# Attention in a four-layer transformer sequence: softmax sums as columns of the values matmul, division by query

## The reference

```python
attn = jnp.einsum('bhnd,bhsd->bhns', q, k) * SCALE
attn = jax.nn.softmax(attn, axis=-1)
o = jnp.einsum('bhns,bhsd->bhnd', attn, v)
return o.transpose(0, 2, 1, 3).reshape(B, N, D)     # then @ proj_w + proj_b
```

## Time and profile before

| what | value |
|---|---|
| median of 3 runs | 2044.21 us |
| the profiled execution | 2036.93 us |
| its span, first to last instruction | 2035.2 us |
| PE (matmul) busy | 1920.9 us, 94%, 40741 instructions |
| PEld (weight load, beside PE) busy | 1591.5 us, 78% |
| DVE busy | 1685.4 us, 83%, 3915 instructions |
| ACT busy | 1411.7 us, 69%, 3672 instructions |
| POOL busy | 648.7 us, 32% |
| mean granted TensorE clock | 0.994 of full speed |

### The profile page before, as it was taken

The page is one execution under the profiler, slowest core; times in us unless marked ns, Lnnn a source line. Parts: engine busy times, 40 slices in busy tenths (PEclk is TensorE's granted clock), DMA queues, the critical chain, the costliest instruction groups (busy, mean ns, idle before and its releaser), DMA issues.

```text
span 2035.2 us, 93251 instructions
## 1 busy us (share of the span) xinstructions
PE 1920.9 (94%) x40741; PEld 1591.5 (78%) x40741; DVE 1685.4 (83%) x3915; ACT 1411.7 (69%) x3672; POOL 648.7 (32%) x1132
## 2 busy tenths in 40 slices
PE   3789999999999999999999999999999999999998
PEld 2567878887877887878887877887888887777877
DVE  2778888888888898878898888898888888889875
ACT  1455767777776777776777776777776777676777
POOL 1322333333333323333323333333333332323322
PEclk9899999999999999999999999999999999999999
DMA  4200000000000000000000000000000000000000
GB/s 176 53 3 3 16 21 21 21 11 18 21 16 21 21 21 11 19 16 21 21 20 10 20 16 21 21 21 21 9 16 21 21 21 8 21 16 8 3 3 14
DMA packets 48113, 42.97 MB, mean 21 GB/s; under 512 B 12640, under 2 KB 38368, under 8 KB 47456
## 3 DMA queue, kind: packets, MB, share of 16 engines
q1 hardware_dynamic: 47712, 37.02, 6.4%
HBM read 32.54 MB, written 4.46 MB: 18 GB/s over the span
## 4 chain that ended last, share of the span: by engine, by line
PE 79%; DVE 10%; ACT 6%; issue 2%; DMA 1%; POOL 0%; DVEq 0%; ACTq 0%; POOLq 0%
PE bank L967 9%; PE turns L858 8%; PE turns L841 7%; PE turns L862 7%; PE bank L874 6%; PE bank L887 6%; PE bank L904 5%; PE bank L914 5%; PE bank L976 4%; PE bank L897 3%; PE bank L812 3%; PE bank L779 3%; DVE top L1059 3%; PE bank L827 3%; PE bank L816 3%; ACT pT L1203 2%
## 5 line engine op out<-in xcount | busy, mean ns | idle before, releaser
L1203 ACT ACTIVATE pT<-turns 128x512 f32<-128x512 f32 x640 | 330.2, 602 | 165.1 <-PE turns L862 164.7
L738 POOL TENSOR_TENSOR shifted<-moments,eps 128x2 f32<-128x2 f32 x256 | 50.1, 196 | 1127.1 <-DVE moments L1023 1126.5
L1059 DVE TENSOR_REDUCE top<-turns 128x32 f32<-128x2048 f32 x160 | 364.2, 2276 | 44.3 <-PE turns L841 43.6
L1063 DVE RECIPROCAL inv_sum<-bank 128x256 f32<-128x256 f32 x160 | 279.7, 1748 | 39.7 <-PE bank L874 38.6
L858 PE MATMUL turns<-inv_sum,of_keys 32*128 32x128 f32 x5120 | 277.9, 284 | 3.8 <-issue 2.3
L862 PE MATMUL turns<-q_heads,k_heads 32*128 32x128 f32 x5120 | 263.0, 271 | 2.7 <-issue 2.6
L1238 ACT ACTIVATE pT<-bank,mod 128x64 f32<-128x64 f32 x896 | 195.7, 331 | 51.7 <-PE bank L967 50.6
L858 PEld LDWEIGHTS turns<-inv_sum,of_keys 32*128 32x128 f32 x5120 | 206.8, 187 | 30.5 <-ACT inv_sum L1152 13.1
L862 PEld LDWEIGHTS turns<-q_heads,k_heads 32*128 32x128 f32 x5120 | 209.2, 187 | 4.0 <-issue 3.8
L1029 DVE TENSOR_SCALAR n_rows<-x_rows,moments,rstd 128x128 f32<-128x128 f32 x512 | 185.6, 405 | 29.3 <-POOL rstd L740 28.2
L841 PE MATMUL turns<-k_heads,q_heads 32*128 32x128 f32 x5120 | 189.4, 283 | 12.5 <-ACT pT L1203 10.2
(11 more groups left out here) (150 smaller groups left out, 3923.1 us busy)
## 6 DMA issues: line engine op xcount, KB each, us to landing
gates<-gate_store SPq DMA_DIRECT2D x64, 256.0 KB, 4.2
x_rows<-x SPq DMA_DIRECT2D x32, 128.0 KB, 2.1
c_rows<-context SPq DMA_DIRECT2D x32, 128.0 KB, 2.1
out<-x_rows SPq DMA_DIRECT2D x32, 128.0 KB, 1.8
w_sb<-weights SPq DMA_DIRECT2D x1, 2368.0 KB, 12.6
pT<-weights SPq DMA_DIRECT2D x1, 1024.0 KB, 4.9
logit_bias<-logit_store SPq DMA_DIRECT2D x64, 1.5 KB, 3.4
row_sb<-rows SPq DMA_DIRECT2D x1, 769.5 KB, 6.7
```

The lines of the kernel that those rows point to most:

```text
L1059: nc.vector.tensor_reduce(top[s][:, :].rearrange("p (g c) -> p g c", c=32)[:, :, 0:2 * GROUP], turns[:, :, :].rearrange("p g (c k) -> p g ...
L1063: nc.vector.reciprocal(inv_sum[s][:, :], banks.take()[:, 0:TOK]).then_inc(v_emptied, 1)
L1203: nc.scalar.activation(turn_cols[s][:, g, :], by_turn[g][:, :], ACT.Exp, scale=ATT_SCALE).then_inc(scores_read, 1)
```

## The change

- The matrix `own_ones` and the step sums are gone. `v_heads` has the same 1024 columns, cut anew: for every sequence, turn and `lo` one block of 32 columns: values of the head on the upper 64 partitions, values of the head on the lower 64, 8 columns of ones for the upper, 8 of ones for the lower. The ones are written once, in setup.
- A values matmul gives, for 64 columns (queries of one `lo`), the weighted values of two heads and their sums. The two `lo` no longer accumulate; they go to columns of their own, and the bank's 512 columns are all used. Heads change places for this: q is split by slot // 2, k and v by slot % 2.
- DVE turns 32x32 blocks of the whole bank, after which queries are on partitions, takes the reciprocal of 32 columns, multiplies, and turns 128x256 back into `oT`. Out waits for that last one, through the new semaphore `o_turned`. The results lie in `weighed` (the memory of `q_heads`) and `o_rows` (in the place of the old `inv_sum`).
- ACT moves v with two instructions instead of four.
- `SEQUENCE` has 2912 digits, 91 steps a group, in another order throughout.

```diff
-    return [..., ("scores", None), ("sums", None), ("values", None), ("out", a)]
+    return [..., ("scores", None), ("values", None), ("out", a)]
...
-        v_heads = each("v_heads", [D, GROUP * TURNS, 2 * QUAD])
-        inv_sum = each("inv_sum", [D, TOK])
-        low = [i[:, 0:D] for i in inv_sum]
+        v_heads = each("v_heads", [D, GROUP * TURNS * 2, 4 * HD])
+        o_rows = each("o_rows", [D, TOK])
+        inv_sum = each("inv_sum", [D, GROUP * 4, 2])
+        low = [o[:, 0:D] for o in o_rows]
+        weighed = [q[:, :, :, :].rearrange("p g l q -> p (g l q)") for q in q_heads]
...
-                sp.dma_start(own_ones[:, :, :], own_ones_in.rearrange("p (l c) -> p l c", l=2)).then_inc(weights_in, 16)
...
+                for s in range(STREAMS):
+                    pool.wait_ge(consts_made, 3 + STREAMS + 2 * s)
+                    for pair in range(2):
+                        at = HD * (2 + pair)
+                        nc.gpsimd.memset(v_heads[s][SEQ * pair:SEQ * (pair + 1), :, at:at + HD], 1.0).then_inc(consts_made, 1)
...
@@ tensor @@
-                        wv = w(...).rearrange("p (g r c) -> p g r c", g=TURNS, r=2)
+                        wv = w(...).rearrange("p (n r c) -> p n r c", r=2, c=HD)
...
-                    if kind == "sums":
-                        after("pT", s)
-                        dst = to_v.slot()
-                        for lo in range(2):
-                            for g in range(TURNS):
-                                mm = nc.tensor.matmul(dst[QUAD * g:QUAD * (g + 1), 0:TOK], own_ones[:, lo, :], pT[s][:, g, :, lo, :],
-                                                      start=lo == 0, stop=lo == 1)
-                        mm.then_inc(v_filled, 1)
...
                     if kind == "values":
                         after("v", s)
-                        after("pT", s)
-                        dst = to_v.slot()
-                        ready["o", s] = to_v.moved_out()
+                        dst = to_v.slot()[:, :].rearrange("p (b h l q) -> p b h l q", b=GROUP, h=2, l=2)
+                        after("pT", s)
                         for tb in range(GROUP):
                             for lo in range(2):
                                 for g in range(TURNS):
-                                    mm = nc.tensor.matmul(dst[QUAD * g:QUAD * (g + 1), tb * SEQ:(tb + 1) * SEQ],
-                                                          v_heads[s][:, tb * TURNS + g, lo * QUAD:(lo + 1) * QUAD], pT[s][:, g, tb, lo, :],
-                                                          start=lo == 0, stop=lo == 1)
+                                    mm = nc.tensor.matmul(dst[QUAD * g:QUAD * (g + 1), tb, :, lo, :], v_heads[s][:, 2 * (tb * TURNS + g) + lo, :],
+                                                          pT[s][:, g, tb, lo, :].rearrange("p (h q) -> p h q", h=2), start=True, stop=True)
                         mm.then_inc(v_filled, 1)
+                        ready["o", s] = (o_turned, count.seen.setdefault("o", 0) + 1)
...
@@ vector @@
-                    if kind == "sums":
-                        nc.vector.reciprocal(inv_sum[s][:, :], banks.take()[:, 0:TOK]).then_inc(v_emptied, 1)
-                        sums_at[s] = banks.uses
                     if kind == "values":
-                        src = banks.take()
-                        dve.wait_ge(v_emptied, sums_at[s])
-                        nc.vector.tensor_tensor(oT[s][:, :, :].rearrange("p g q -> p (g q)"), src[:, 0:TOK], inv_sum[s][:, :],
-                                                ALU.mult).then_inc(v_emptied, 1)
+                        nc.vector.transpose(weighed[s], banks.take()[:, :]).then_inc(v_emptied, 1)
+                        dve.wait_ge(v_emptied, banks.uses)
+                        by_query = weighed[s].rearrange("p (n c) -> p n c", c=4 * HD)
+                        own_result(nc.vector.reciprocal(inv_sum[s][:, :, :], by_query[:, :, 2 * HD:4 * HD:HD]))
+                        own_result(nc.vector.tensor_tensor(o_rows[s][:, :].rearrange("p (n a d) -> p n a d", a=2, d=HD),
+                                                           by_query[:, :, 0:2 * HD].rearrange("p n (a d) -> p n a d", a=2),
+                                                           inv_sum[s][:, :, :].unsqueeze(3).broadcast_to([D, GROUP * 4, 2, HD]), ALU.mult))
+                        nc.vector.transpose(oT[s][:, :, :].rearrange("p g q -> p (g q)"), o_rows[s][:, :]).then_inc(o_turned, 1)
...
@@ scalar, kind "v" @@
-                            for lo in range(2):
-                                at = lo * QUAD + (2 * pair + lo) * HD
-                                m = nc.scalar.activation(v_heads[s][part, :, at:at + HD],
-                                                         src[part, 0:TOK].rearrange("p (n l d) -> p n l d", l=2, d=HD)[:, :, lo, :],
-                                                         ACT.Identity)
+                            m = nc.scalar.activation(v_heads[s][part, :, HD * pair:HD * (pair + 1)],
+                                                     src[part, 0:TOK].rearrange("p (n d) -> p n d", d=HD), ACT.Identity)
```

More of the change, by code:

```diff
@@ L134, in attention @@
     return [("q", a), ("k", a), ("v", a), ("tops", None), ("lows", None), ("scores", None),
-            ("sums", None), ("values", None), ("out", a)]
+            ("values", None), ("out", a)]
 def mlp(m):
@@ L174 @@
[L174 to L178, removed]
@@ L199 @@
[L199 removed]
+    "0010002101200012100311310100201102300200130011021012010110100100010030010011030311101200120210100101"
+    "0210102212120212100022001020210101201022113320132300022132201132302102320310233120320014240110421404"
+    "1301243434022001203121303304014034110224221334402140200343142413044231432143032133220141303142200124"
+    "2101432421331344013240330422143031114113402034241104132240204203403112301231420301233230232040413130"
@@ new lines @@
+    "2401410031024134320414213124021223040202024003134141203322340221314430414213024342230104343113103321"
+    "3421104442103121003313024021313431201341240143042302124320403012024033410413420414024142342410312302"
+    "0201314024231423124234002130140233120320014240110421404130124343402200120312130330401403411022422133"
+    "4402140200343142413044231432143032133220141303142200124210143242133134401324033042214303111411340203"
+    "4241104132240204203403112301231420301233230232040413130240141003102413432041421312402122304020202400"
@@ new lines @@
+    "3134141203322340221314430414213024342230104343113103321342110444210312100331302402131343120134124014"
+    "3042302124320403012024033410413420414024142342410312302020131402423142312423400213014023312032001424"
+    "0110421404130124343402200120312130330401403411022422133440214020034314241304423143214303213322014130"
+    "3142200124210143242133134401324033042214303111411340203424110413224020420340311230123142030123323023"
+    "2040413130240141003102413432041421312402122304020202400313414120332234022131443041421302434223010434"
@@ new lines @@
+    "3113103321342110444210312100331302402131343120134124014304230212432040301202403341041342041402414234"
+    "2410312302020131402423142312423400213014023312032001424011042140413012434340220012031213033040140341"
+    "1022422133440214020034314241304423143214303213322014130314220012421014324213313440132403304221430311"
+    "1411340203424110413224020420340311230123142030123323023204041313024014100310241343204142131240212230"
+    "4020202400313414120332234022131443041421302434223010434311310332134211044421031210033130240213134312"
@@ new lines @@
+    "0134124014304230212432040301202403341041342041402414234241031230202013140242314231242340021301402331"
+    "2032001424011042140413012434340220012031213033040140341102242213344021402003431424130442314321430321"
+    "3322014130314220012421014324213313440132403304221430311141134020342411041322402042034031123012314203"
+    "0123323023204041313024014100310241343204142131240212230402020240031341412033223402213144304142130243"
+    "4223010434311310332134211044421031210033130240213134312013412401430423021243204030120240334104134204"
@@ new lines @@
+    "1402414234241031230202013140242314231242340021301402331202134040202404401310213134001210423214133023"
+    "0341334024113212342003402342103314023133410143423214001242123024241001322113042032111300144200424333"
+    "0113004204143023420014300232130440314413044132131432401311310431310404143014123434410421130410241230"
+    "1110013401014340401304420121441401420101240221041002134002413401021141301200103413204031400013103140"
+    "3410213131130411004203010401413011401410414101332144010410441411034100310101011001001012140140114411"
@@ L200 @@
+    "311311011111"
 )
@@ L220, in bank_uses @@
         "kvnorm": (1, 0) if modulated else (0, 1), "q": (1, 0), "k": (0, 1), "v": (0, 1),
-        "lows": (0, 1), "sums": (1, 0), "values": (1, 0),
+        "lows": (0, 1), "values": (1, 0),
```

(6 more changed lines are left out.)

38 lines of the change are left out of this document (7 added, 31 removed).

## The result

The changed kernel takes 1972.32 us (median of 4 runs, 1962.4 to 1977.46) against 2043.06 us for the kernel before (median of 4, with one more run than the three shown ahead): a ratio of 0.965, 95% interval 0.9605 to 0.9693, 71 us less. It lies inside the range of 1880 to 1985, 47 us above the forecast of 1925. The profiled execution took 1973.59 us, with a span of 1970.7, 64.5 less than before.

A forecast was written before the change was run, and what follows sets the result against it. PE bounds, DVE right behind. PE's 138 us less gave span 1897; capping DVE's 1642 us at 87.9% gave 1914, profiled 1916, plus 7 to the median 1923, rounded up to 1925 us; range 1880 to 1985.

The forecast's parts named there:

- DVE's prices: Four new DVE instructions per attention: 0.69 + 0.35 + 0.51 + 0.42 = 1.97 us, against 2.17 for the two removed.
- one-pass rate: DVE's block transposes were priced like plain one-pass moves, 1.03 ns a column past the first 128.
- rival 3: Slow DVE transposes, two passes a column, 128 us more: slower than before, about 2068 us; chance 0.07.
- PE's 138 us: Removing the sums matmuls saves PE 0.86 us in each of 160 attentions, 138 us; upper end 171.
- has nothing to give: In a steady 300 us the clock was fully granted, so no gain or loss was priced for it.
- the 240 us of waits: Main phase beyond PE's 1748 us of dense work: about 240 us, taken as waits that five streams do not cover.
- DVE fell by 16.5 us, not 32: DVE's work was to fall by 0.20 us in each of 160 attentions, 32 us, to 1642 in the main phase.
- a reader of one SBUF tensor is never stretched: On DVE beside POOL: L1020, reading one SBUF tensor, never passes 0.297 us, while L1037 reaches 1.239.
- ACT's v moves: In the v step, four moves at 0.267 us become two at 0.395: 1.07 becomes 0.79, 45 us less on ACT.
- if no in-order engine here gets past 87.9%: DVE's main-phase share capped at PE's dense share: 1642 / 0.879 = 1868 us, span 1914.
- Rival 2: DVE's queue exposed: PE waits 0.4 to 0.5 us more per attention, 60 to 80 us; about 1985 us; chance 0.16.
- So the order fits the longer DVE tail: Between values and out, the new stream order leaves median 3.2 us of other PE work, against 2.6 before.

The follow-up runs named there:

- dead sums: Changed kernel with the 8 sums matmuls put back on PE ahead of each values step, read by nobody: 2068.93 us, ratio 1.012 to the kernel before.
- equally fitted orders: Kernel before and changed kernel, each with a stream order found by the same search for its own step durations: 2057.94 us and 1986.83 us.

## Why the prediction was right or wrong

**Right: the direction, the sums as the source, DVE's prices.** The reciprocal of 256 columns and the sums group are gone, and the dead sums show that the gain is theirs. The four new instructions take 0.706, 0.353, 0.475 and 0.446 us, 1.98 in all, where 1.97 was forecast (0.69, 0.35, 0.51, 0.42). The one-pass rate held for the block transposes, so rival 3 is dead. The Trainium skill's page "Vector Engine (DVE) Microarchitecture Reference", section 3.8, gives one element per cycle per lane for the transpose. The trace agrees: from 446 ns for 256 columns to 706 ns for 512 it is 1.02 ns a column, the rate of the one-pass rows before. The multiply ran from 424 to 953 ns around a median of 425, as the row of L1037 had suggested.

**Mis-sized: PE's 138 us were 118.** The prediction named less than 120 us as a sign of being wrong, and this one came. It said of the clock that it "has nothing to give", from one steady stretch, and put it at nothing. But the changed kernel lost more of it: the mean granted clock was 0.985 in its profiled execution and 0.994 in that of before, that is, some 58 us at 1.2 GHz against some 23. PE was busy in 47.2 us of the one and 14.0 us of the other. At 1.2 GHz the same step takes nearly twice as long. In this piece of the chain of the changed kernel the clock goes back to full within the third line (0.50 from 209.1 to 212.4, then 1.00; start us, us, what):

```profile
211.45 0.43 PE turns L868 x8
211.88 0.43 PE turns L864 x8
212.31 0.34 PE turns L868 x8
212.65 0.22 PE turns L864 x8
212.87 0.22 PE turns L868 x8
```

As an estimate, half of the 33 us more at the low clock, some 15 us, is what the clock added to PE's busy time, most of the missing 20.

The prices of the steps held. A step's price depends on the tile shape of the step ahead of it, in both kernels alike. In the chain of the changed kernel:

```profile
1220.00 0.43 PE bank L818 x2
...
1224.37 0.58 PE bank L833 x32
1224.95 0.89 PE bank L882 x64
1225.85 1.10 PE turns L847 x32
1226.95 1.93 PE bank L963 x8
1228.88 0.44 PE bank L893 x4
1229.32 1.73 PE bank L963 x8
```

Behind v, which is 32 columns wide too, values take 0.89 us, so the output in runs of 32 costs nothing. L963 takes 1.93 us behind tops and 1.73 behind a step of its own shape. Behind a 128x128 matmul values take 1.03 us (first fence, the changed kernel), and so did the sums of before take 1.00 instead of 0.86 (second fence, the kernel before):

```profile
1024.60 0.43 PE bank L818 x2
1025.03 1.03 PE bank L882 x64
```

```profile
1016.33 0.11 PE bank L849
1016.43 1.00 PE bank L874 x16
1017.44 0.89 PE bank L887 x64
```

There 1.00 + 0.89 become 1.03, 0.86 less: the price that I took, whichever of the two steps pays for the change of shape. Counted over both whole strings, the changes of shape nearly cancel. Steps of full tiles behind smaller ones rise from 445 to 468, at 0.15 to 0.20 us each. Steps with 32 columns behind another shape fall from 330 to 307, at 0.14 each. What is left of the 20 us lies near the waits: the changed code in the old order, with 91 us more of PE idle time than in the new one, shows PE busy 1828.6 us, 26 more, of which the clock explains some 5 as an estimate. How the rest splits was not tried.

**Misread: the 240 us of waits.** They are 1989 us less the 1748 of dense steps. PE was busy 1920.9 - 14.5 = 1906 us of the main phase, so about 83 us were idle, and the other 158 are matmuls that took longer than their dense price.

**Mis-sized: DVE fell by 16.5 us, not 32.** The tail is as priced (317 us of 347 are spent again, 30 less). But the norm's L1025 (L1029 before) grew from 185.6 to 201.3 us with the same 512 instructions (durations in ns, min/median/max, columns as in the earlier trace rows):

```profile
L1025 DVE TENSOR_SCALAR n_rows<-x_rows,moments,rstd x512: 304/343/1086, 49.6 to 1945.9; 128x128 f32<-128x128 f32 x171
```

The prediction took from L1020 that a reader of one SBUF tensor is never stretched. L1025 reads one SBUF tensor, beside its per-row factors, and reaches 1086 ns (1083 before). The neighbour is GpSimd: in the changed kernel the 262 of these instructions with no POOL instruction beside them took at most 348 ns, while the 250 with one took 546 ns on average; before, 199 had one. What grew is the number beside POOL's long additions over 256 or 512 columns, from 100 to 147, at 0.69 us each instead of 0.34: some 16 us as an estimate.

**Mis-sized: ACT's v moves.** 45 us were forecast from 4 x 0.267; busy time fell only from 138.6 to 121.0. Means of overlapping instructions were added (1.07 us per attention) where the group's busy time, 0.87 us, was the right figure.

**Wrong: the step "if no in-order engine here gets past 87.9%".** It made DVE's share the limit and gave 1914 for the span. It set DVE's busy share beside PE's share of dense work; PE's own busy share of that phase was 1906 of 1989 us, 95.8%, so the trace never showed 87.9% as a limit of busy time. DVE's work in the changed kernel (1669 less some 11, in 1925 us) is 86.1%, and in the same order two kernels with 120 and 219 us less of DVE work are only 11 and 12 us faster. What the missing gain turned into is 54 us more of PE idle time, for normed rows (+21), exps (+7), k (+7), maxima (+5) and others. At equally fitted orders PE's idle time rises by the same 53 us, so it is not the given order alone that makes it; without the division it falls by 34 there. So DVE's work does bear on it, through waits spread over many steps and not through a cap on its share. How much of the 54 us each cause has stays open. Rival 2 had the size (1985) with the wrong wait: maxima are 5 us of the 54. That the time still lies in the range is in part luck: the upper end stood at 1985 for rival 2's sake, and the step that gave 1925 did not hold.

**Wrong by omission: the order as a side remark.** "So the order fits the longer DVE tail" was right, but I gave it no price. It is the largest term: the code alone, in the old order, is 45 us slower than before, and the new order is worth 117 to it. Counting the gaps (median 2.6 against 3.2 us, a tenth under 1.0 against 2.1) had pointed at the place, L893, without a size. Still, the change is no mere reordering: at equally fitted orders it is worth 71 us.

## What to carry to other kernels

Where every engine walks one written order, price an edit twice. In the old order saved work can turn mostly into waits (11 us gained for 42 here). With a fitting order more of it counts (71 us for 118 of PE, 48 for 120 of DVE). An edit tried without its order can measure slower and still be good. Take a matmul step's price from a place in the chain with the same neighbours, and compare busy time of groups, not means, where instructions overlap. Compare the mean granted clock of both kernels before explaining what is left.

## What the runs showed of the hardware

Some changes of tile shape between neighbouring matmul steps cost time: 0.14 us into a step of 32 columns (values, 1.03 against 0.89) and 0.15 to 0.20 us from a smaller tile into a full one (L963, 1.93 against 1.73). Tops took 1.10 us whatever stood ahead of it. With 330 and 445 such places in the kernel before, this is 110 to 135 us of it as an estimate, which no group shows.

A DVE instruction with one SBUF tensor as input, the norm's 128x128 with per-row factors, took up to 1086 ns beside GpSimd and at most 348 without it; the transpose in SBUF stayed at 445 to 448 ns throughout.

The granted clock had part in the spread. Four executions of the changed kernel took 1962.4, 1971.06, 1973.59 and 1977.46 us at mean clocks of 0.993, 0.989, 0.985 and 0.982. It is lost mainly while the streams start up (one 30 us stretch of the changed kernel, then of the kernel before, columns as in the earlier trace rows):

```profile
110.00:140.00 30.00, 23.55 (x522) 18.70 (x525) 22.47 (x46) 14.14 (x28) 8.19 (x13) 0.90 0.01 2
```

```profile
110.00:140.00 30.00, 24.89 (x610) 20.44 (x603) 25.39 (x50) 13.55 (x31) 7.42 (x14) 1.00 0.01 3
```

The first is of the changed kernel, PE busy 23.55 us and the clock at 0.90 on average, that is, part of the stretch at 1.2 GHz; the second of the kernel before, 24.89 us and full clock. That a less busy PE is what loses the clock is not shown: without division, in the fitted order, PE was busy 216.9 us between 46 and 300, more than the changed kernel's 211.5, and the mean clock there was 0.90 against 0.93.
